# Graph network kernel: another order of loads, one-hot units and small products ahead of its batch loop

## What is computed

```python
x, src, dst = ...                      # (1250, 512), 21250 edges, sorted by dst
h = max(layernorm(x), 0)
hW = h @ W + b_w                       # first layer: attention over the edges
e = leaky_relu((hW @ a[:D])[dst] + (hW @ a[D:])[src] + b_a)
alpha = exp(e) / segment_sum(exp(e), dst)[dst]
x = x + segment_sum(alpha * hW[src], dst)
h = max(layernorm(x), 0)
x = x + mixture_of_graph_experts(h)    # second layer: four experts of two layers, two per node
```

## Time and profile before

| what | value |
|---|---|
| median of three runs | 807.62 us (807.48 to 807.95) |
| the profiled execution | 807.52 us, of which its span is 805.7 us |
| PE busy in the span | 763.8 us (95%) |
| DVE, ACT, POOL busy | 395.5, 278.4, 120.5 us |
| DMA | 125.55 MB, mean 156 GB/s |

### The profile page before, as it was taken

One profiled execution on the slowest core, in us unless ns is written; L12 is line 12 of the kernel. 1 busy time (PEld: TensorE's weight loads), 2 busy tenths in 40 slices (PEclk: granted clock), 3 DMA queues, 4 the chain that ended last, 5 costly groups with the idle time before them and its releaser, 6 DMA issues.

```text
span 805.7 us, 11768 instructions
## 1 busy us (share of the span) xinstructions
PE 763.8 (95%) x3755; PEld 620.2 (77%) x3755; DVE 395.5 (49%) x978; ACT 278.4 (35%) x569; POOL 120.5 (15%) x135
## 2 busy tenths in 40 slices
PE   4779999999899999999999999899999999999993
PEld 2368886888788888777777777688888888888882
DVE  6778889889752448721624325323223323322320
ACT  6755666655643431511513213122122211211210
POOL 4000000000000001840000000231332322322211
PEclk9999999999999999999999999999999999999997
DMA  5100000321411147799697864599427964449900
GB/s 155 73 2 3 4 4 1 111 79 62 151 40 54 58 118 239 218 335 342 187 380 266 305 225 130 189 276 353 116 67 220 302 218 116 97 118 269 333 11 6
DMA packets 46741, 125.55 MB, mean 156 GB/s; under 512 B 7252, under 2 KB 7384, under 8 KB 46665
## 3 DMA queue, kind: packets, MB, share of 16 engines
q1 hardware_dynamic: 27375, 78.40, 29.3%
q0 software_dynamic: 9488, 26.95, 13.1%
q10 hardware_dynamic: 9802, 19.19, 7.6%
HBM read 72.21 MB, written 53.20 MB: 156 GB/s over the span
## 4 chain that ended last, share of the span: by engine, by line
PE 88%; DMA 5%; DVE 3%; ACT 1%; issue 1%; POOL 0%; ACTq 0%; SPq 0%; POOLq 0%; DVEq 0%
PE ps L1545 17%; PE ps L1546 17%; PE ps L1547 17%; PE ps L1910 6%; PE ps L1909 6%; DMA xs<-in_x 4%; PE ps L1604 4%; PE ps L1837 3%; PE ps L1775 3%; PE ps L1776 3%; PE ps L1920 1%; PE ps L1881 1%; PE ps L1692 1%; PE ps L1661 1%; PE ps L1663 1%; PE ps L1662 1%
## 5 line engine op out<-in xcount | busy, mean ns | idle before, releaser
L1910 PE MATMUL ps<-slots,CTs 125*128 x230 | 90.9, 395 | 0.0
L1909 PE MATMUL ps<-slots,CTs 125*128 x207 | 81.5, 394 | 0.0
L1473 DVE CAST CTs<-ps 125x512 fp32r<-125x512 f32 (+1 forms) x69 | 37.3, 596 | 84.8 <-PE ps L1837 57.8
L1380 DVE TENSOR_TENSOR he_t<-ps,b_b 125x512 f32<-125x512 f32 x40 | 27.5, 691 | 103.6 <-PE ps L1547 71.8
L913 ACT ACTIVATE slots<-he_t 125x512 fp32r<-125x512 f32 x40 | 25.4, 636 | 150.2 <-DVE he_t L1380 126.8
L1518 DVE TENSOR_TENSOR tm<-ps,b_b 128x512 f32<-128x512 f32 x23 | 15.9, 692 | 103.8 <-PE ps L1547 103.8
L638 POOL DMA_INDIRECT out<-tg,rec x23 | 36.9, 1605 | 193.7 <-ACT tg L963 176.9
L1545 PE MATMUL ps<-W,agT_hi 128*125 128x512 f32 x160 | 63.5, 397 | 0.0
L1545 PE MATMUL ps<-W,h2T_hi 128*125 128x512 f32 x160 | 63.4, 396 | 0.0
L1547 PE MATMUL ps<-W,agT_lo 128*125 128x512 f32 x160 | 63.3, 396 | 0.0
L1546 PE MATMUL ps<-W,agT_hi 128*125 128x512 f32 x160 | 63.2, 395 | 0.0
(11 more groups left out here) (300 smaller groups left out, 1751.8 us busy)
## 6 DMA issues: line engine op xcount, KB each, us to landing
he_d<-slots SPq DMA_DIRECT2D x30, 448.0 KB
slots<-he_d SPq DMA_DIRECT2D x30, 448.0 KB
w_d<-slots SPq DMA_DIRECT2D x3, 4096.0 KB, 18.6
slots<-w_d SPq DMA_DIRECT2D x24, 512.0 KB
t_d<-he_t SPq DMA_DIRECT2D x40, 224.0 KB
c_d<-c_nat SPq DMA_DIRECT2D x10, 546.9 KB
raw<-in_L_gnn_Wl ACTq DMA_DIRECT2D x4, 1024.0 KB
raw<-in_L_gnn_Wr ACTq DMA_DIRECT2D x4, 1024.0 KB
```

Source lines behind the costliest of these rows:

```text
L1380: v.tensor_tensor(he_t[:, n % 4, :], ps[0:P, bank_of(x, g, t), :], b1_b[:, x % 2, :], ALU.add).then_inc(pre_ready.sem, 1)
L1473: v.tensor_copy(CTs[:, 4 * r:4 * r + n, :], ps[0:P, r, 0:n * S].rearrange("p (c n) -> p c n", n=S)).then_inc(cts_ready.sem, 1)
L1909: mm(o, CTs[:, t, :], part(k, P, t * 1024, P), start=False, stop=False)
L1910: last = mm(o, CTs[:, t, :], part(k, P, t * 1024 + D, P), start=False, stop=t == T - 1)
```

## The change

It touches the prelude and one product of the batch loop.

- **Loads.** x is loaded in four transfers, all by SP: rows 0 to 111 and rows 112 to 124 of the first five tiles, then the same of the other five (`x_in`, `x_late_in`; `CUTS` was there before). W0 follows them on SP's queue and the gate bias is last. ACT's queue keeps the destinations only. `W0_f` lies elsewhere in memory.
- **One-hot units.** Three pairs of banks in place of two, so unit u waits for the eviction of unit u - 3. DVE evicts units 2 and 11, ACT the other twenty.
- **Chunk tables.** DVE's table chain no longer stands behind four source vectors. `sum_tables` moves behind unit 7, and its second half, `turn_tables`, stands behind unit 8.
- **Row statistics** are spread between DVE's table steps.
- **The rest of the dense side** moves back: the split of W0 on ACT behind the first `norm`; the ten source and bias vectors on DVE behind the one-hot comparisons of batch 0; `W0_lo` and the low bias part behind its first `hT_lo`. PE waits for them inside batch 0, where they are used, and no longer ahead of it.
- **Tables of functions.** A square root of one number (`spark`) at ACT's start loads the table that `std` needs later.
- **Bias.** `bw_2` and `ones_2` have 128 rows in place of 33; the added rows of `bw_2` are zero.

```diff
-        W0_f = at("W0_f", [128, KC, D], F32, 34016)
+        W0_f = at("W0_f", [128, KC, D], F32, R1 + 10240)
...
-        bw_2 = early("bw_2", [33, D], F32R)
-        ones_2 = early("ones_2", [33, P], F32R)
+        bw_2 = early("bw_2", [128, D], F32R)
+        ones_2 = early("ones_2", [128, P], F32R)
...
+        HOT_DVE = (2, 11)
+        HOT_ACT = tuple(u for u in range(NU) if u not in HOT_DVE)
...
-            sp.dma_start(xs[:, 0:T // 2], x_v[:, 0:T // 2]).then_inc(x_in.sem, 16)
+            for m in CUTS:
+                sp.dma_start(xs[m, 0:T // 2], x_v[m, 0:T // 2]).then_inc(x_in.sem, 16)
+            for m in CUTS:
+                sp.dma_start(xs[m, T // 2:], x_v[m, T // 2:]).then_inc(x_late_in.sem, 16)
+            sp.dma_start(W0_f[:], W0.rearrange("(c k) d -> k c d", k=128)).then_inc(w0_in.sem, 16)
             sp.dma_start(gb_b[:], gate_b.partition_broadcast(P)).then_inc(vec_in.sem, 16)
...
-            link(g.memset(spark[:], 0.0))
...
             act.sem_inc(window_out.sem, window_out.start)
             edges_of(act, 1, dst)
-            act.dma_start(W0_f[:], W0.rearrange("(c k) d -> k c d", k=128)).then_inc(w0_in.sem, 16)
-            act.dma_start(xs[:, T // 2:], x_v[:, T // 2:]).then_inc(x_in.sem, 16)
+            act.wait_ge(*spark_ready(1))
+            a.activation(spark[:], spark[:], ACT.Sqrt).then_inc(spark_ready.sem, 1)
...
-                             ps[0:P, u % 2 * 2:u % 2 * 2 + n // m, 0:m * P], ACT.Relu).then_inc(hot_ready.sem, 1)
+                             ps[0:P, u % 3 * 2:u % 3 * 2 + n // m, 0:m * P], ACT.Relu).then_inc(hot_ready.sem, 1)
...
-                hot_columns(u)
+                if u in HOT_ACT:
+                    hot_columns(u)
                 if u == 3:
                     act.wait_ge(*rows_turned(1))
                     copy(e_gc[:], ps[0:P, 7, 0:CG * CR]).then_inc(cols_ready.sem, 1)
-                if u == 9:
-                    act.wait_ge(*w0_in(16))
-                    copy(W0_hi[:], W0_f[:]).then_inc(w0_hi_ready.sem, 1)
                 if u == 10:
-                    act.wait_ge(*small_in(48))
-                    act.wait_ge(*small_ready(1))
-                    copy(bw_2[0:1, :], bw_b[0:1, :]).then_inc(bw_hi_ready.sem, 1)
-                if u == 12:
                     act.wait_ge(*tab_ready(1))
                     columns(0)
-                if u == 18:
+                if u == 14:
                     act.wait_ge(*var_ready(1))
                     a.activation(std[:], std[:], ACT.Sqrt).then_inc(std_ready.sem, 1)
-                    act.wait_ge(*norm_ready(1))
-                    norm(0)
+            act.wait_ge(*norm_ready(1))
+            norm(0)
+            act.wait_ge(*w0_in(16))
+            copy(W0_hi[:], W0_f[:]).then_inc(w0_hi_ready.sem, 1)
+            act.wait_ge(*small_in(48))
+            act.wait_ge(*small_ready(1))
+            copy(bw_2[0:1, :], bw_b[0:1, :]).then_inc(bw_hi_ready.sem, 1)
...
+                    act.wait_ge(*spark_ready(2))
                     a.activation(spark[:], spark[:], ACT.Exp)
...
                                            accum_out=wa_f[:, c, w:w + 1]).then_inc(wa_f_ready.sem, 1)
 
-            dve.wait_ge(*w0_in(16))
-            dve.wait_ge(*small_in(48))
-            source_vectors(0)
+            def hot_columns(u):
+                dve.wait_ge(*hot_made(u + 1))
+                v.tensor_scalar(onehot_p[:, u * CU:(u + 1) * CU, :].rearrange("p (h c) n -> p h (c n)", h=2),
+                                ps[0:P, u % 3 * 2:u % 3 * 2 + 2, 0:CU // 2 * P], 0.0, None, ALU.max
+                                ).then_inc(hot_dve_ready.sem, 1)
+
+            def row_stats(tiles):
+                for t in tiles:
+                    last = v.bn_stats(x_stats[:, t, :], xs[:, t, :])
+                return last
+
+            dve.wait_ge(*x_in(32))
+            row_stats(range(0, 2))
+            hot_columns(HOT_DVE[0])
             dve.wait_ge(*spans_spread(1))
             link(v.tensor_scalar(g_b[:], ps[0:NW, 6, CG * CR:CG * CR + NCH], w_lo[:], float(W - 1), ALU.subtract, ALU.is_le))
...
             v.tensor_scalar(tab_f[:, 1:2], tab_f[:, 1:2], -1.0, None, ALU.add).then_inc(n_ready.sem, 1)
+            row_stats(range(2, 3))
             dve.wait_ge(*n_summed(1))
             v.tensor_copy(tab_f[:, 2:3], ps[0:NW, 7, 0:1]).then_inc(tab_f_ready.sem, 1)
+            row_stats(range(3, 4))
             dve.wait_ge(*tab_turned(1))
...
             v.tensor_scalar(tab_b[0:1, :, BW], tab_m[:], 1.0, None, ALU.min).then_inc(tab_ready.sem, 1)
 
 
-            source_vectors(1)
-            for w in range(2):
-                dve.wait_ge(*wa_f_ready(2 * KC - 1 + w))
-                v.scalar_tensor_tensor(spill[w][0:P, :], bw_b[:], 1.0, a_b[0:P, w, :], ALU.mult, ALU.mult,
-                                       accum_out=ab[:, w:w + 1]).then_inc(ab_ready.sem, 1)
-            dve.wait_ge(*x_in(32))
-            for t in range(T):
-                last = v.bn_stats(x_stats[:, t, :], xs[:, t, :])
...
+            dve.wait_ge(*x_late_in(32))
+            link(row_stats(range(T // 2, T)))
             for t in range(T):
...
-            dve.wait_ge(*ab_ready(2))
-            v.tensor_scalar(s_add[:], ab[:, 0:1], ab[:, 1:2], ba_c[:], ALU.add, ALU.add).then_inc(wa_ready.sem, 1)
-            dve.wait_ge(*std_ready(1))
-            link(v.reciprocal(rstd[:], std[:]))
-            v.scalar_tensor_tensor(shift[:], x_mv[:, :, 0], -1.0, rstd[:], ALU.mult, ALU.mult).then_inc(norm_ready.sem, 1)
             dve.wait_ge(*vec_in(16))
+
+            def scales():
+                dve.wait_ge(*std_ready(1))
+                link(v.reciprocal(rstd[:], std[:]))
+                v.scalar_tensor_tensor(shift[:], x_mv[:, :, 0], -1.0, rstd[:], ALU.mult, ALU.mult
+                                       ).then_inc(norm_ready.sem, 1)
+
+            def sources():
+                dve.wait_ge(*w0_in(16))
+                dve.wait_ge(*small_in(48))
+                source_vectors(0)
+                source_vectors(1)
+                for w in range(2):
+                    dve.wait_ge(*wa_f_ready(2 * KC - 1 + w))
+                    v.scalar_tensor_tensor(spill[w][0:P, :], bw_b[:], 1.0, a_b[0:P, w, :], ALU.mult, ALU.mult,
+                                           accum_out=ab[:, w:w + 1]).then_inc(ab_ready.sem, 1)
+                dve.wait_ge(*wa_f_ready(2 * KC))
+                link(v.tensor_copy(wa[:, :, 0:2], wa_f[:]))
+                v.tensor_tensor(wa[:, :, 2:4], wa_f[:], f32(wa[:, :, 0:2]), ALU.subtract).then_inc(wa_ready.sem, 1)
+                dve.wait_ge(*ab_ready(2))
+                v.tensor_scalar(s_add[:], ab[:, 0:1], ab[:, 1:2], ba_c[:], ALU.add, ALU.add).then_inc(wa_ready.sem, 1)
+
+            def first_weights_low():
+                dve.wait_ge(*w0_hi_ready(1))
+                v.tensor_tensor(W0_lo[:], W0_f[:], f32(W0_hi[:]), ALU.subtract).then_inc(w0_lo_ready.sem, 1)
+                dve.wait_ge(*bw_hi_ready(1))
+                v.tensor_tensor(bw_2[32:33, :], bw_b[0:1, :], f32(bw_2[0:1, :]), ALU.subtract).then_inc(bw_lo_ready.sem, 1)
 
             def one_hots(slot, w, first):
...
                 if b > 0:
                     product_low(b - 1)
+                else:
+                    scales()
+                    sources()
                 turned_low0(b)
+                if b == 0:
+                    first_weights_low()
                 if b == T - 1:
                     source_sums(0, T - 2)
                 with dve.If(more):
...
+            def evicted(u):
+
+                if u in HOT_DVE:
+                    pe.wait_ge(*hot_dve_ready(HOT_DVE.index(u) + 1))
+                else:
+                    pe.wait_ge(*hot_ready(HOT_ACT.index(u) + 1))
...
-                if u > 1:
-                    pe.wait_ge(*hot_ready(u - 1))
+                if u > 2:
+                    evicted(u - 3)
...
-                if u == 6:
+                if u == 7:
                     sum_tables()
+                if u == 8:
+                    turn_tables()
...
+                if b == 0:
+                    pe.wait_ge(*tab_ready(1))
...
                 if b > 0:
                     pe.wait_ge(*hT_lo_ready(b))
                 else:
-                    pe.wait_ge(*wa_ready(2))
-                    pe.wait_ge(*tab_ready(1))
+                    pe.wait_ge(*hot_ready(len(HOT_ACT)))
+                    pe.wait_ge(*hot_dve_ready(len(HOT_DVE)))
                 pe.wait_ge(*h_ready(b + 1))
...
+                if b == 0:
+                    pe.wait_ge(*wa_ready(2))
                 for c in range(KC):
...
                 if b > 0:
                     pe.wait_ge(*hw_lo_ready(b))
+                else:
+                    pe.wait_ge(*w0_lo_ready(1))
+                    pe.wait_ge(*bw_lo_ready(1))
                 o = ps[0:P, 6, :]
                 mm(o, ones_2[:], bw_2[:], start=True, stop=False)
                 for c in range(KC):
...
-            pe.wait_ge(*hot_ready(NU))
-            pe.wait_ge(*w0_lo_ready(1))
```

(22 more changed lines are left out.)

11 lines of the change are left out of this document (5 added, 6 removed).

## The result

| | before | changed |
|---|---|---|
| median, first comparison | 807.73 us (807.48 to 807.95) | 799.02 us (797.63 to 802.81) |
| ratio | | 0.990 (95%: 0.986 to 0.994) |
| the profiled execution | 807.52 us | 802.81 us, span 801.0 |
| mean granted clock of the runs | 0.991 | 0.983, 0.986, 0.991, 0.991 |

The forecast was 800.0 with 796.4 to 802.0, and the median lies in it: 1% less time. The profiled execution is the slowest of the four and has the lowest clock, so its trace can show falls of the clock that the others do not have; theirs were not kept.

What follows compares the result with a forecast made beforehand. The prediction took the prelude's chain (x, DVE's row statistics), then PE narrowly in the loop, as the bound. Gains 6.1 + 1.3 + 0.2 = 7.6 took 807.6 to 800.0 us; own range 799.0 to 801.0, overall 796.4 to 802.0.

Steps and rivals of the forecast that it cites:

- The prelude up to unit 11: Prelude: PE starts about 9.1, twelve units take 10.8, small products and tables 4.0, so unit 11 is ready at 24.
- the third pair: One-hot units: with three pairs of banks 0.9 per unit; with two, two units take 2.3, ACT waiting 0.40 for PE.
- DVE from there: DVE's work summed from unit 11 at 24.0 to the end of batch 1's `hT_lo` at 53.9, against 60.0 now.
- The 0.9 of the table row: Batch loop, ahead of DVE's comparisons: 0.90 is the table row's load, no wait, and stays; DVE alone needs 7.14 per batch.
- the gain at the end of `hT_lo` of batch 1 (6.1): Prelude through batch 1: DVE reaches the end of `hT_lo` at 53.9 instead of 60.0, a gain of 6.1 us.
- the bias edit: Batch loop: 128 bias rows save PE 0.35 per batch, 7.31 to 6.95; rival of no effect, 800.6, inside the 0.52 forecast range.
- The 0.06 for its own load: Batch loop: the bias product's own weight load is likely not hidden either, so 0.35 per batch was taken instead of 0.29.
- the 0.29 forecast for the two steps behind it: Batch loop: two steps around the bias product, 0.42 and 0.33, are 0.29 more than twice 0.23; this excess goes.
- 1.3: Batches 1 to 9: DVE becomes the bound, eight batches at 7.14 in place of 7.31, a gain of 1.3 us.
- The end of the loop: Loop end: PE no longer comes 0.95 after `hT_lo`, but a DVE tile ready some 0.25 ahead limits the gain to 0.2.
- The clock: Rival, chance 0.07: PE's 2 us wait in batch 0 halves the clock through batch 1's counts, giving 803, range 801.5 to 804.
- the counter-evidence I used: In the rival of a vanished half-clock stretch: idle stretches of 1.4 us elsewhere in the trace left the clock at full.

Runs made afterwards that it cites:

- e4: Changed kernel plus eight spare products of 500 columns into a free bank during PE's wait for `W0_lo` in batch 0: median 797.58 us, ratio 0.988 to the kernel before.

## Why the prediction was right, and where it was not

**The prelude up to unit 11** held: PE's first product at 9.03 (9.1), x in time, the table chain without a stall at `L1625`, unit 11 at 24.27 (24.0), its eviction 1.20 (1.2). Inside it the size of the third pair was off: 2.0 and not 3.0 of the 14.9.

**DVE from there** held: comparisons of batch 0 at 31.38 (31), W0's product at 46.90 (46.7) with a wait of 1.97 (2), and without a fall of the clock its end at 49.99 (49.8).

**The 0.9 of the table row is the step that failed.** I put down that it is no wait, that it stays, and that DVE alone needs 7.14. Its loads run beside DVE's work: batch 1 of e4 goes from 46.79 to 53.00 and shows DVE's own need, 6.21. Two terms hung on it. I took the gain at the end of `hT_lo` of batch 1 (6.1), but DVE does not hold PE there: PE's batch 0 ends 7.9 earlier (57.88 to 49.99), a number I had (49.8 against 57.9) and set aside, and that is the prelude's gain. And the loop keeps PE as its bound at 7.02, so all of the bias edit arrives.

**The bias edit** gave 0.29 per batch (7.31 to 7.02) and not 0.35. The 0.06 for its own load was there: the step ahead went from 0.18 to 0.11. Of the 0.29 forecast for the two steps behind it only 0.20 came, since the first of them stays at 0.32 and does not reach 0.23; why it does is open. Instead of 1.3 the loop gave 2.7 from batch 0's end to the bias product of the last batch.

**The end of the loop** was to give 0.2 and took about 0.5. PE's pause ahead of the product behind the loop was 1.40 and is 1.79 in e4.

**The clock** was a rival at 0.07, with 803. The profiled execution took 802.81, and in both traces of the changed kernel a fall comes in PE's pause or just behind it. It was no rival but part of the likeliest case. That 803 and 802.81 are so close is in part luck: the fall ended at 52.72, ahead of batch 1's counts, and cost 2.6 at batch 0's end (52.58 against 49.99), and this run had the fall at 120.99 and a longer one at 213 besides. The rival's mechanism was named, a pause of 2 us in mid-batch; the counter-evidence I used was of other pauses, of 1.4 us, and said nothing of this one.

So the sum was 7.9 + 2.7 - 0.5 = 10.1 (9.8 at equal clock), less about 2 for the clock, and not 6.1 + 1.3 + 0.2. The 800.0 lies close by luck: two missed terms, 2.2 to 2.5 too little of gain and 2 of clock, nearly cancel. The forecast's 0.2%, 1.6 us, as what a measurement can tell was too fine as well, as the 42 runs of the kernel before show.

## What to carry to other kernels

Idle time ahead of an instruction that follows loads of registers is not a cost of that place: look where the sequencer's last wait ended, and compare a batch in which the engine was late. When an edit opens a pause on PE of about 2 us, price the product behind it at the half clock as well as at the full, or fill the pause with products into a free bank. Compare kernels at equal mean clock before giving a part its share of a gain.
